# Taking 22 tiles out of the gathers of two passes: self-loop rows picked by VectorE behind the one-hots of pass one

## The reference

```
edge_index = stack([src, dst])
x = layernorm(x + L0(x))      # 4 times: h = relu((x + sum x[src] -> dst) @ W1 + b1) @ W2 + b2
x = layernorm(x + L1(x))      # relu(x @ root + bias + sum over 8 types of mean (x @ W[type])[src] -> dst)
x = layernorm(x + L2(x))      # w_rel = comp @ weight (16 of them); alpha[16] from a small network;
                              # relu(sum alpha[type16] * (x @ w_rel[type16])[src] -> dst  + indegree * x @ update)
x = layernorm(x + L3(x))      # gate * (x @ W[type8] + b)[src] -> dst, relu(sum + x @ loop_weight)
```

## Time and profile before

| | |
|---|---|
| median of the runs | 2252.14 us (2251.11 to 2255.48) |
| the profiled execution | 2252.56 us, of which span 2250.8 us |
| busy | TensorE 65%, GpSimd 60%, VectorE 40%, ScalarE 27% |
| granted TensorE clock, mean | 0.802 |
| gathers at L1013 | 416 of pass one, 832 of passes two and three |

### The profile page before, as it was taken

How to read it: one execution, slowest core, us unless ns; L and a number is a source line. 1 busy time by engine, 2 the same in 40 slices (tenths; PEclk the granted TensorE clock), 3 DMA queues, 4 the chain that set the end, 5 groups by cost and what they waited for, 6 DMA issues and landing times.

```text
span 2250.8 us, 31616 instructions
## 1 busy us (share of the span) xinstructions
PE 1463.2 (65%) x7538; PEld 989.7 (44%) x7539; DVE 906.3 (40%) x2269; ACT 599.7 (27%) x1689; POOL 1360.4 (60%) x1574
## 2 busy tenths in 40 slices
PE   4776999999987777777764655555455433434433
PEld 2332554545456665666653533343333333323333
DVE  7887122213673444444445533333344212212212
ACT  3776000000023333333331644444343000000000
POOL 5000166720007777777777777777777777777775
PEclk8888999999988989989897876667677756565565
DMA  1000011100213333333333222222222222222221
GB/s 31 0 0 10 15 9 12 11 3 0 59 54 109 94 113 112 95 112 110 95 113 97 72 81 79 71 80 79 71 81 84 56 56 56 55 56 56 55 56 46
DMA packets 126652, 137.49 MB, mean 61 GB/s; under 512 B 80706, under 2 KB 97866, under 8 KB 123433
## 3 DMA queue, kind: packets, MB, share of 16 engines
q0 software_dynamic: 40896, 81.94, 13.9%
q1 hardware_dynamic: 85673, 54.54, 8.1%
HBM read 91.88 MB, written 44.52 MB: 61 GB/s over the span
## 4 chain that ended last, share of the span: by engine, by line
POOL 50%; PE 21%; issue 18%; ACT 5%; DVE 2%; ACTq 1%; DMA 1%; POOLq 1%; SPq 0%; DVEq 0%
POOL adj L1013 49%; PE acc L1315 18%; ACT adj L1714 5%; PE misc L1251 1%; PE acc L1586 1%; PE acc L1202 1%; ACTq L1707 1%; DVE adj L2607 0%; DMA adj<-table,adj 0%; DVE adj L2606 0%; ACTq L1714 0%; POOLq L1009 0%; PE acc L1251 0%; ACT adj L1773 0%; PE acc L1204 0%
## 5 line engine op out<-in xcount | busy, mean ns | idle before, releaser
L1013 POOL DMA_INDIRECT adj<-table,adj x832 | 793.5, 954 | 253.6 <-issue 252.9
L1586 PE MATMUL acc<-adj 128*128 x1760 | 364.5, 385 | 499.7 <-DMA adj<-table,adj 253.3
L1586 PEld LDWEIGHTS acc<-adj 128*128 128x128 f32 x1760 | 328.5, 285 | 560.3 <-issue 560.2
L1013 POOL DMA_INDIRECT adj<-tablex,adj x416 | 392.8, 944 | 210.9 <-issue 126.5
L1773 ACT ACTIVATE adj<-adj 128x128 f32<-128x128 f32 x832 | 264.5, 390 | 581.0 <-DMA adj<-tablex,adj 315.2
L1315 PE MATMUL acc<-adj,feat 128*128 (+1 forms) x2100 | 406.8, 354 | 8.4 <-issue 8.4
L1513 PE MATMUL acc<-adj 128*128 128x128 f32 x1664 | 245.3, 310 | 124.1 <-ACT adj L1773 113.9
L1997 DVE TENSOR_TENSOR adj<-acc,drel 128x768 f32<-128x768 f32 (+1 forms) x148 | 139.9, 948 | 423.6 <-PE acc L1586 423.3
L1513 PEld LDWEIGHTS acc<-adj 128*128 128x128 f32 x1664 | 228.8, 220 | 167.2 <-issue 167.1
L1315 PEld LDWEIGHTS acc<-adj,feat 128*128 (+1 forms) x2100 | 186.2, 98 | 217.1 <-issue 13.1
L959 POOL TENSOR_TENSOR node_rep<-node_rep,compb 128x128 f32<-128x128 f32 x128 | 58.5, 457 | 272.4 <-DMA node_rep<-in_L_gnn_weight_dram 263.5
(11 more groups left out here) (352 smaller groups left out, 1297.6 us busy)
## 6 DMA issues: line engine op xcount, KB each, us to landing
table<-adj SPq DMA_DIRECT2D x24, 1024.0 KB, 4.1
adj<-table,adj POOLq DMA_INDIRECT x834, 2.5
table<-adj SPq DMA_DIRECT2D x25, 512.0 KB, 2.9
adj<-tablex,adj POOLq DMA_INDIRECT x416, 2.5
table<-adj SPq DMA_DIRECT2D x25, 64.0 KB, 2.0
out_dram<-adj SPq DMA_DIRECT2D x24, 64.0 KB, 1.5
temp<-in_x_dram SPq DMA_DIRECT2D x4, 256.0 KB, 3.1
wrel<-node_rep SPq DMA_DIRECT2D x16, 64.0 KB
```

Of the source, the lines that this page charges most:

```text
L1013: pool.indirect_dma_start(ring[:, p_, 0:D], None, rows_, bass.IndirectOffsetOnAxis(ap=gidx[:, p_:p_ + 1], axis=0)).then_inc(msgs_in[third_ ...
L1586: last = nc.tensor.matmul(acc[:, bass.ds(blk[s], width)], hot[:, c, j, :], ring_flat[:, bass.ds(place[s], width)], start=False, stop=True, ...
```

## The change

For 22 of the 25 blocks (the third to the 24th) the self-loop edges are no longer gathered in passes two and three. The edges of one tile per block (the eighth of its turn) are put into the places that the self-loops of the block leave, and that tile is skipped: by the gathers, by ScalarE's weights and by TensorE's matmuls. So each of passes two and three gathers 394 tiles.

What the self-loops add is made from the block itself, since their source is their target: VectorE picks, for each node, of the 16 rows of its block in `stage` the one of its self-loop's type. In pass one that is `own_rows`, 16 chained operations per block (one multiply, 15 multiply-adds of 128x128), all behind the one-hots of a turn; two calls, for the last two picked blocks, stand in the calls behind the pass's last turn. The result stays in SBUF and is added in `block_sum` of pass two with one operation. For pass three `table_parts` of pass two has 8 such operations per block behind the gated rows.

To find which edge goes where, layers 0 to 2 of L0 get new work: VectorE `code_lists`, `loop_nodes`, `loop_eighths` and `loop_holes`; GpSimd four more plain DMAs (two of them, `here_i` and `behind_i`, of 128x22 separate 4-byte elements), three rounds of 22 gathers (`found_rows`) and 44 scatters (`filled`); SyncE a copy from DRAM to DRAM, 11 clears of lists and later their 22 loads. VectorE puts the result into the edges' tables at the third turn of pass one (`edges_moved`, `loops_taken`). In the setup SyncE has three more loads of `dst`, a wait for all of them and a small store ahead of its next loads, GpSimd one more tensor operation and VectorE three, for one more check.

GpSimd's order in L0 is another: slices 0 to 3, 22 gathers, 4 to 6, 22 gathers, 7 and 8, 22 gathers, 22 scatters, slices 9 to 12, 22 scatters, the pads, the 28 scatters of edges, slices 13 to 15. SyncE's share of the slices per layer is 4, 3, 6 and 3 where it was 6, 5, 5 and none.

The diff, cut to its core:

```diff
-LATE_FLAGS, LATE_SUMS, LATE_READ, PLACES_SET = 1, 2, 3, 4
+LATE_FLAGS, LATE_SUMS, LATE_READ, LISTS_SET, NODES_SET, PLACES_SET, EIGHTS_SET, HOLES_SET = range(1, 9)
+LB, LN = 2, BLOCKS - 3
+EMPTY_AT = 7
-EARLY_SLICES = (range(0, 6), range(6, 11), range(11, 16), ())
+EARLY_SLICES = (range(0, 4), range(4, 7), range(7, 13), range(13, 16))
-ENDS_IN = 6 * 16
+ENDS_IN = 9 * 16
...
+            sp.dma_start(next1_i[0:EVENQ, :], bass.AP(dst.tensor, dst.offset + 1, [[TW, EVENQ], [1, TW]])).then_inc(ends_in, 16)
...
+            hold(sp, ends_in, ENDS_IN)
+            sp.dma_start(first_list, firsts_i).then_inc(ends_in, 16)
             sp.dma_start(compb[:, :, :], g2comp.partition_broadcast(P)).then_inc(comp_in, 16)
...
+                sp.dma_start(eighths[0:TILES - 1, :].rearrange("t e -> (t e)"), bass.AP(dst.tensor, dst.offset, [[P // 16, (TILES - 1) * (P // 8)], [1, 1]])
+                             ).then_inc(ends_in, 16)
+                sp.wait_ge(late_counted, LISTS_SET)
+                for g in range(KINDS_OF_LIST):
+                    sp.dma_start(by_place(holes[g]), no_hole.bitcast(I32).rearrange("p (h i) -> p h i", h=LISTS)).then_inc(ends_in, 16)
                 layers(False)
-                sp.wait_ge(edges_out, SWAPPED * 16)
-                sp.dma_start(moved[:, :, :], edges0.rearrange("(t p) w -> p t w", p=P)).then_inc(edges_in, 16)
...
-                    for j in range(SIZES[c]):
+                    for j in range(SIZES[c] - (1 if c == 1 and emptied(ph, u) else 0)):
                         p_ = place_of(ph, u, c) + j
                         pool.indirect_dma_start(ring[:, p_, 0:D], None, rows_,
...
+                for k, o in ((0, here_i), (1, behind_i)):
+                    pool.dma_start(o, bass.AP(dst.tensor, dst.offset + emptied_tile(0) * P + k, [[1, P], [TPT * P, LN], [1, 1]])).then_inc(edges_in, 16)
...
+                slices(0, 4)
+                pool.wait_ge(late_counted, NODES_SET)
+                found_rows(lambda b: sixteen[:, b, :], lambda b: eighths, row_i)
+                slices(4, 7)
...
+                filled(0)
+                slices(9, 13)
...
+                filled(1)
+                pads()
+                for n in range(SWAPPED // 4):
+                    edges_part(n)
+                slices(13, 16)
                 passes(False)
...
+                    if own:
+                        own_rows(before, 0, R2)
...
+                if ph == 2 and not general and emptied(2, b):
+                    nc.vector.scalar_tensor_tensor(y1[:, :], loop_rows[:, bass.ds(b.num(1, 1 - LB), 1), :].rearrange("p b o -> p (b o)"),
+                                                   w2[:, bass.ds(b.num(1, TILES - LB), 1)], y1[:, :], ALU.mult, ALU.add).then_inc(picked, 1)
...
+            def own_rows(b, lo, hi):
...
+                for r in range(lo, hi):
+                    rows_ = stage[:, b.r, r * D:(r + 1) * D]
+                    of_r = own_kind2[:, bass.ds(b.num(1, 1 - LB), 1), r:r + 1].rearrange("p b r -> p (b r)")
+                    if r == 0:
+                        ins = nc.vector.tensor_scalar(mine, rows_, of_r, None, ALU.mult)
+                    else:
+                        dve.wait_ge(picked, b.num(R2, r + (1 - LB) * R2))
+                        ins = nc.vector.scalar_tensor_tensor(mine, rows_, of_r, mine, ALU.mult, ALU.add)
+                    ins.then_inc(picked, 1)
...
+                    if not general:
+                        hold(dve, rows_set, b.num(1, 1))
+                        hold(dve, prod_free[SIDE], blocks_seen(2, b, 1))
+                        for r in range(R3):
...
+                            nc.vector.scalar_tensor_tensor(own, stage[:, b.r, r * D:(r + 1) * D],
+                                                           own_kind3[:, bass.ds(b.num(), 1), r:r + 1].rearrange("p b r -> p (b r)"), own,
+                                                           ALU.mult, ALU.add).then_inc(picked, 1)
```

More of the change, by code:

```diff
@@ L409, in gnn @@
         zerob = sb("zerob", [P, KB], BF16)
+        hole = zerob[:, :].bitcast(F32)
+        here_i, behind_i, slot_c, slot_d, row_i, node_i, found = (hole[:, i * LN:(i + 1) * LN].bitcast(I32) for i in range(7))
+        here_f, node_f, tile_f, place_n, ends_f = (hole[:, i * LN:(i + 1) * LN] for i in (0, 7, 8, 9, 10))
+        more_f, many_f = (place_f[:, i * LN:(i + 1) * LN] for i in range(2))
+        loop_i = late[:, 2 * SWAPPED:2 * SWAPPED + LN].bitcast(I32)
+        assert 11 * LN <= KB // 2 and LN <= SWAPPED and 2 * LN <= 4 * 15
         epst = sb("epst", [P, 1])
@@ L655, in tiles_from, with by_place, emptied, picks @@
             return u.num(TPT, PARTS_AT[c])
-        def msgs_before(ph, u, c):
-            uses = sum(uses_in(q, third_of(ph, u), c) for q in range(1, ph))
-            return u.third(16 * SIZES[c], 16 * SIZES[c] * uses)
+        def by_place(list_):
+            return list_.rearrange("(h p i) z -> p h (i z)", h=LISTS, p=P)
+        def emptied(ph, u):
+            return ph > 1 and (not isinstance(u.k, int) or LB <= u.num() < LB + LN)
+        def picks(b):
+            return not isinstance(b.k, int) or LB - 1 <= b.num() < LB + LN
+        def full_turns(r):
+            return sum(1 for i in (*range(LB), *range(LB + LN, TURNS)) if i % AHEAD_T == r)
+        def tiles_in_pass(ph, r, c):
+            n = uses_in(ph, r, c)
+            if ph == 1 or c != 1:
+                return n * SIZES[c]
+            return n * (SIZES[c] - 1) + full_turns((r - ph + 1) % AHEAD_T)
+        def msgs_upto(ph, u, c):
+            before = sum(tiles_in_pass(q, third_of(ph, u), c) for q in range(1, ph))
+            if ph == 1 or c != 1:
+                return u.third(16 * SIZES[c], 16 * (before + SIZES[c]))
+            full = full_turns(u.r) - (1 if u.r == (TURNS - 1) % AHEAD_T and not u.last() else 0)
+            return u.third(16 * (SIZES[c] - 1), 16 * (before + SIZES[c] - 1 + full))
         def uses_in(ph, r, c):
@@ L1035, in released @@
                     for c in range(len(SIZES)):
-                        for _ in range(uses_in(ph, r, c)):
-                            pool.sem_inc(msgs_in[r][c], 16 * SIZES[c])
+                        for i in range((r - ph + 1) % AHEAD_T, TURNS if c < 2 else TURNS - 1, AHEAD_T):
+                            pool.sem_inc(msgs_in[r][c], 16 * (SIZES[c] - (1 if c == 1 and emptied(ph, At(0, i)) else 0)))
             def table_written(ph, general):
@@ L1062, in of_pairs, with pads @@
                                             bass.IndirectOffsetOnAxis(ap=fidx[:, n:n + 1], axis=0)).then_inc(xe_in, 16)
-            def passes(general):
+            def pads():
                 pool.wait_ge(low_free, 1)
@@ L1101, in _, with slices @@
             with pool.Else():
[L1102 to L1112, removed]
-                    weights_slice(LAYERS - 1, q)
+                def slices(n, upto):
+                    for z in range(n, upto):
+                        weights_slice(z // (SLICES // LAYERS), z % (SLICES // LAYERS))
@@ L1769, in take @@
                     return
-                hold(act, msgs_in[third_of(ph, u)][c], msgs_before(ph, u, c) + 16 * SIZES[c])
-                for j in range(SIZES[c]):
+                hold(act, msgs_in[third_of(ph, u)][c], msgs_upto(ph, u, c))
+                for j in range(SIZES[c] - (1 if c == 1 and emptied(ph, u) else 0)):
                     o = ring[:, place_of(ph, u, c) + j, 0:D]
@@ L2285, in layers @@
                 for l in range(LAYERS):
+                    if l == 0 and not general:
+                        code_lists()
                     if l == 1 and not general:
@@ L2370, in body @@
                         kind_hots(t, 2)
+                    if isinstance(t.k, int) and t.num() == LB:
+                        edges_moved()
+                        for q, t_, n, _ in HOMES:
+                            nc.vector.tensor_copy(idx8[:, t_:t_ + n], moved_i[:, q:q + n, 1])
+                        loops_taken()
                     if b.exists():
@@ L2373, in body @@
                     if before.exists():
-                        table_parts(1, before)
+                        table_parts(1, before, now=False)
+                    own = before.exists() and picks(before)
                     if b.exists():
@@ L2459, in table_parts @@
                     nc.vector.tensor_copy(own, acc[:, SIDE_AT[1]:SIDE_AT[1] + D]).then_inc(prod_free[SIDE], 1)
+                    if not general and picks(b) and now:
+                        own_rows(b, 0, R2)
                 else:
@@ L2511, in one_pass @@
                 if ph < 3:
-                    table_parts(ph, last.plus(-1))
-                    table_parts(ph, last)
+                    table_parts(ph, last.plus(-1), general)
+                    table_parts(ph, last, general)
             n_count = [0]
```

271 lines of the change are left out of this document (244 added, 27 removed).

## The result

The changed kernel takes 2357.86 us (2357.30 to 2359.05), the kernel before on the same chip 2251.62 us; the ratio is 1.0469, with a 95% interval from 1.0451 to 1.0487. It is 4.7% slower, where 2.1% was forecast, and lies above the range. The direction and the place were right; a cost of some 50 us wasn't in the sum.

A forecast was written before the change was run, and what follows sets the result against it. GpSimd's gather issue was taken to bound the three passes, TensorE L0. From 2252.56 us, -55.2 + 72.6 + 3 + 6 + 5 + 5 + 10 = +46.4 gave 2299 us, 2% slower; 8-in-10 range 2262 to 2345.

The forecast's parts named there:

- GpSimd's line in L0: GpSimd's summed work in L0, including 110 gathers and scatters at 1.265 us, 139.2 us; last slices end at 648.4.
- near_in behind the slices: Layer 3: near_in issued at 649.3 behind slices 13 to 15, 75.9 us later; TensorE stands 72.6 us ahead of the carries.
- first rival: Layer 3: near_in isn't late and TensorE has no stall, so the kernel is faster, 2223 us; chance 0.08.
- Start of GpSimd's line: L0: GpSimd's new work begins behind code_lists at 289.8 us; four plain DMAs bring it to 298.
- second rival: GpSimd in L0: element DMAs cost 20.8 us each, its line ends 36 us later, 2335 us; chance 0.12.
- Setup: Setup: SyncE's extra loads, store and hold plus VectorE's three check operations cost 3 to 9 us, taken as +6.
- Gathers: Passes two and three: 22 fewer gathers each, at 1.261 and 1.249 us, save 55.2 us.
- Borders: Pass borders: own_rows behind pass one and 8-operation picks behind pass two cost 5 us each, bounds 11 and 6.4.
- Picks in pass one: VectorE in pass one: own_rows, 16 chained operations at 0.40 us, 6.4 us a turn, fits idle time; cost 0.
- third rival: Pass one: VectorE sets the turn, 2.1 us more in each of 23 turns, 48 us, 2347 us; chance 0.13.
- Gathers beside VectorE's chains: Passes one and two: some 190 gathers slowed beside VectorE's new chained operations, +10 us, bounds 0 and 18.
- Clock behind the idle time: Layer 3: TensorE may run slowly for a while when it starts again after the stall, +3 us.

The follow-up runs named there:

- e4: Changed kernel with each 4-byte code written as a 64-byte row of its own (16 copies), no two writes sharing 64 bytes: 2306.62 us.
- e5: Changed kernel with codes still written as 4 bytes, but each 64 bytes from the next: 2307.10 us.
- e1: Changed kernel with SyncE's loads from near_in to pass one's weights ahead of slices 13 to 15, x's pad moved up: 2290.27 us.
- e6: Changed kernel with near_in ahead of slices 13 to 15 and codes as 64-byte rows: 2241.16 us, 0.993 of the kernel before.
- e7: Changed kernel with only the setup altered: SyncE's hold, first_list store and eighths copy behind the weights and x loads: 2343.68 us.
- e10: Changed kernel with near_in ahead of the last slices, 64-byte code rows and early lists, repeated: 2232.86 us, 0.9918 of the kernel before.
- e9: Changed kernel with near_in early, 64-byte code rows, early lists, and border picks behind the table's last rows: 2223.28 us, 0.9872 of the kernel before.

## Why the prediction was wrong

The step that failed is the pricing of GpSimd's line in L0: "Three rounds of 22 gathers and 44 scatters: 110 x 1.265 = 139.2. With some 2 us for waits on landings". A scatter was priced by its issue, taken from the 28 scatters of 16 bytes before, and its landing at no more than a part of these 2 us. The issue was right. Behind the code scatters DMA stood or crawled for some 28 us, twice: the first pause cost GpSimd 26 us and TensorE 22.5 in layer 2 (its chunks are 17.9 us later than before ahead of it and 40.4 behind), the second GpSimd 27.75. Taken away they give back 52.3 us of the first gather (814.24 in the kernel after, 761.92 in e4). What is left is 49.0 us (e4) and 51.2 us (e5) above the kernel before on the same chip, where I had 46.4.

That the rest comes so near the forecast is in part luck. Up to the first gather e4 is 93.2 us later than the kernel before, where the sum had 72.6 + 3 + 6 = 81.6; the three passes of the kernel after are 40.7 us shorter, where the sum had 55.2 - 10 - 10 = 35.2. The two errors cancel by half.

Point by point:

- **near_in behind the slices.** Right in place, and e1 and e6 show that the order on SyncE is its cause. The price, 70.13 us without pauses against 72.6, is right with some luck: in e4 `near_in` goes out at 667.02, not 649.3, but TensorE too comes to the carries late, at 620.04 (690.17 - 70.13) and not 599.40, and the two delays cancel. (The terms of the low bound add up to 69.3, not 68.8, which changes nothing.) The first rival falls.
- **Start of GpSimd's line.** My 289.8 and 298 became 304.84 and 318.42. Of the first 15 us some 10.7 are the setup, and 5 the longer idle time of VectorE in layer 0 (8.47 us against 3.66) that I didn't have (e7). The wait of 9.40 us for the 11 clears ahead of `firsts_b` was not in the sum either.
- **Element DMAs.** The two of 2816 elements took 2.76 us together, 1.4 each, where I had 2.7 each and feared 20.8. The second rival falls. The Trainium skill ("DMA: Bandwidth & Descriptors", Anatomy of one DMA), by which many descriptors show little in the time, agrees with this 1.4.
- **Setup.** 10.7 us (219.84 to 230.56) where I had 6 and a bound of 9. How it divides between the hold, the loads and the check is not shown (e7 to e10).
- **Gathers.** GpSimd, passes two and three, to be set beside the earlier trace rows:

```profile
L1112 POOL DMA_INDIRECT adj<-table,adj x349 | 335.0, 960 | 106.3 <-issue 105.1 <-ACT adj L1892 1.2
...
L1112 POOL DMA_INDIRECT adj<-table,adj x369 | 348.4, 944 | 112.4 <-issue 105.7 <-ACT adj L1892 6.7
```

  The price of one is what it was (1.264 and 1.249 us), so 22 fewer are worth 27 to 28 us a pass. Right.
- **Borders.** 9.40 and 3.56 us, where I had 5 each with bounds of 11 and 6.4; e9 shows the picks as their cause.
- **Picks in pass one.** The fifteen chained operations took up to 7.3 us, here in a turn of VectorE in the kernel after:

```profile
1095.34 0.28 DVE L2749 TENSOR_SCALAR feat<-adj,feat 128x128 f32 x1
1095.78 7.29 DVE L2752 SCALAR_TENSOR_TENSOR feat<-adj,feat 128x128 f32 x15 [0.16 <-DVE feat L2749]
```

  So it was in 12 of the 23 turns, 0.49 us a step; in the 11 others the fifteen took some 5.8 us, 0.39 a step, as the 0.40 of the sum. Either way it is hidden: pass one shows no wait of GpSimd within it, and takes 521.5 us against 519.2. The third rival falls.
- **Gathers beside VectorE's chains.** I took 10 us; the 416 gathers of pass one were busy 394.3 us against 391.9, so 2.4, and in pass two a gather took 960 ns where it had 956, some 1.6 us in all. Short operations of 128x128 did much less here than those of 128x416 in the earlier trace rows. The Trainium skill ("SBUF — State Buffer", Who interferes with whom) would have had 19 us by my reading of it; the measurement decides against that use of it.
- **Clock behind the idle time.** 24 matmuls took 7.04 us at 743.70 against 5.34 usually, 1.7 of the 3 that I had. The granted clock was 0.50 in the idle time from 700 to 743 and 0.74 from 743 to 751.

## What to carry to other kernels

Price a DMA by its issue and by its landing, and for a write ask where its neighbours go: here runs of scatters with 128 4-byte writes into adjacent words of DRAM were followed by some 28 us in which the stores and loads of another queue stood or crawled too. When several engines go idle at once and no wait is named, look at the DMA rows of that stretch. And when work is added ahead of a fixed order, follow each queue to the first thing that stands behind it: here three small stores on SyncE, each waiting for GpSimd, held TensorE for 70 us, and moving loads past them left 2.55 of it (e4, e6).

## What the runs showed of the hardware

- Runs of 11 scatters with 128 neighbouring 4-byte writes each were followed by pauses of about 28 us, in which DMA moved 0 to 7 GB/s in the kernel after; with the same writes 64 bytes apart there was none (2357.86 us with a kernel before of 2251.62, against 2307.10 with one of 2255.95).
- In a pause engines stood with no wait to be named: in the first, TensorE for up to 7.28 us at a time (busy for 2.50 of the 10 us from 550 to 560) and VectorE for 23.85; in the second, GpSimd for 27.75.
- A plain DMA from GpSimd with 2816 separate 4-byte elements was issued in 1.4 us, where a gather of 128 rows took 0.94.
